# A graph layer and a mixture of 64 experts on one core: tokens laid 32 to a partition, z made by two engines, beta added to the adjacency chunk on the Pool

## The chip, the core and the metric

The kernel runs on one core of one Trainium2 chip. The metric is the device time of one execution in microseconds (us), and lower is better. A profiled execution gives a trace beside it. Engines are named PE (TensorE), DVE (VectorE), ACT (ScalarE), POOL (GpSimd) and SP (SyncE, which here only issues DMAs).

## The reference

`x` is 4096 tokens of 128 floats, `adj` is 4096 by 4096 floats.

```python
z = (x - mean(x)) / sqrt(var(x) + 1e-5)
scale = 1 / (adj.sum(1) + beta)
x = x + (scale[:, None] * (adj @ z + beta[:, None] * z)) @ kernel + bias
z1 = the same normalisation of x
logits = z1 @ Wr + br                      # 64 experts
top2, index = top_k(logits, 2)
gates = softmax(top2)
x = x + sum over the two experts e of gate[e] * (relu(z1 @ W1[e] + b1[e]) @ W2[e] + b2[e])
```

The hidden width is 256. All of it is float32; the two choices of a token decide which experts it goes to.

## The kernel before, in words

**Tiles.** 4096 tokens are 32 tiles of 128. Tile t holds tokens 128t to 128t+127, one to a partition. Four tiles are a group g (8 groups). The adjacency comes as 8 x 8 chunks of 1 MB, `adj_t[g, k]`: for the 512 target tokens of group g, the 512 source tokens of tiles 4k to 4k+3. A ring of 5 slots holds them (`load_chunk`, L324). SP waits until the chunk five before is used, and then loads the next.

**Group 0 (L847).** The layer norm of x goes first. DVE does it in steps of 4 or 8 tiles (`norm_x`, L590: statistics, a root by ACT, then one tensor_scalar a tile, L600). The last column of z is set to 1, so that the same product also sums the rows of adj. PE runs the chunks of group 0 as float32 products (`whole_chunk`, L825) as tiles of z come.

**Groups 1 to 7.** Of each group's eight chunks, seven are split. ACT rounds the chunk to `high` (`round_chunk`, L494), DVE makes the rest, `low` (`low_part`, L610, instruction L615), and PE runs three products with z_hi and z_lo (`split_chunk`, L833). There are three buffers for high and low. The eighth is a `whole_chunk`. Between the chunks of group g, PE does the rest of group g-1 by a list of places in `step`, L855: `gnn` behind tile 2, `turn_z1` at 16, `router` at 20, `ranks` at 26.

**The own product.** beta times z is added as four 128x128 products of `zi` (a copy of the group's z) with `diag` (identity times beta), behind the group's chunks (`own_product`, L819). POOL makes both (`own_rows`, L434, instructions L437 and L438), two groups ahead.

**DVE's order in group g (L674 on).** residual(g-1), low_part 3, shifts(g-1), low_part 4, 5 and 6, choose(g-1), low_part 0 of the next group, place(g-1), low_parts 1 and 2 of the next. `choose` (L640) finds the two experts and the one-hot `mask`, `place` (L658) the row numbers (`slot`, L667) from the ranks that PE has made and the counts of the tokens already seen.

**ACT's order in group g.** copy_agg(g-1), round_chunk 3, root, 4, normalise(g-1) (z1 into `payload`, L516), 5, copy_z1t, 6, then 0 to 2 of the next group.

**POOL's order.** Constants; per group the bias into x (`add_bias`, L419) and z_lo (`low_z`, L424); own_rows(0) and own_rows(1); then for each g own_rows(g+2) and dispatch(g). `dispatch` (L441) copies z1 for the second choice, waits for the pads and the slots, issues 8 indirect DMAs (L451) that scatter the tokens' rows to the experts' places in `rows`, waits until they have landed, and frees one of two payload buffers.

**Pads.** SP writes the first 128 rows of each expert's place with a row that is marked as no answer: 8 DMAs between chunk loads of groups 1 and 2 (`PADS`, L353), the last behind chunk (2, 6). No scatter starts before all have landed (`prefilled`).

**The rest.** A list of (expert, rows) tiles is made (L692 on), then 92 tiles of 128 rows go through the two expert products (L891 on), answers are scattered back to HBM and gathered in the tokens' order, scaled by the gates and written (L770, L775, L580).

```python
for g in range(GROUPS):
    if g + 2 < GROUPS:
        own_rows(g + 2)
    dispatch(g)
```

## Time and profile before

| | us |
|---|---|
| median of 3 runs | 433.78 (432.93 to 433.87) |
| the profiled execution | 433.03 |
| its span in the trace | 431.2 |
| PE busy | 359.3 |
| DVE busy | 312.4 |
| POOL busy | 250.3 |
| ACT busy | 157.8 |

Times inside the trace count from the span's start. Busy times of engines overlap, so none of them is the length of a stage; the end of a stage is set by the wait that ends last in it. "Idle before" of a row names who ended it. PEclk is the clock granted to TensorE as a part of full speed.

### The profile page before, as it was taken

Reading aid. Unit: us, or ns where it says so; the run is one execution under the profiler, and the core shown is the slowest. Engines: PE = TensorE matmul, PEld = TensorE weight load, DVE = VectorE, ACT = ScalarE, POOL = GpSimd, SP = SyncE. Lnnn points to the kernel's source line nnn. Section 1 sums busy time; section 2 is a strip of 40 time slices with the busy share of each in tenths; the row PEclk is TensorE's granted clock in tenths of the full one; section 3 lists DMA queues with packets and bytes.
Section 4 is the critical chain, followed back from the end, with each engine's and each line's share of the span. In section 5 each row is a group of like instructions: output and inputs, shape, how many; then the busy total and the mean of one; then the engine's idle time right before and its main releaser. Section 6 shows DMA issues by size and latency. Waiting matters only on the chain.

```text
span 431.2 us, 8273 instructions
## 1 busy us (share of the span) xinstructions
PE 359.3 (83%) x2029; PEld 286.2 (66%) x2029; DVE 312.4 (72%) x891; ACT 157.8 (37%) x242; POOL 250.3 (58%) x226
## 2 busy tenths in 40 slices
PE   5899699996999999999899935289999999999300
PEld 2334486784786877868678632179999999999300
DVE  2699779859789798898897628246777767677257
ACT  1115185454384654845738030001222112122054
POOL 4377600308488585884857763517777777777700
PEclk8799899996999999999999975869999999999955
DMA  8998999899696996969955110479999999997189
GB/s 267 351 423 280 338 364 357 240 361 397 249 397 218 420 366 234 401 214 403 374 218 238 44 46 19 142 205 269 307 295 311 304 285 312 295 277 235 31 288 297
DMA packets 59653, 119.32 MB, mean 277 GB/s; under 512 B 7656, under 2 KB 36604, under 8 KB 51440
## 3 DMA queue, kind: packets, MB, share of 16 engines
q1 hardware_dynamic: 41968, 95.95, 63.8%
q10 hardware_dynamic: 12672, 14.58, 11.0%
q0 software_dynamic: 4992, 8.54, 5.5%
q8 instruction: 9, 0.15, 0.1%
q14 instruction: 12, 0.10, 0.1%
HBM read 104.09 MB, written 16.78 MB: 280 GB/s over the span
## 4 chain that ended last, share of the span: by engine, by line
PE 33%; POOL 19%; DVE 17%; DMA 15%; issue 10%; ACT 3%; SPq 1%; ACTq 0%; POOLq 0%; DVEq 0%
POOL dispatched_rows L451 14%; PE bank L897 8%; DMA dispatched_rows<-payload,slot 7%; PE bank L907 4%; PE bank_pair L907 4%; DVE z_sb L600 4%; DVE adj_low L615 3%; POOL diag L438 3%; DMA x_sb<-x 3%; DMA expert_answers<-adj_ring,ans 3%; PE bank L891 2%; PE bank L843 2%; PE bank L839 2%; PE bank_pair L904 2%; PE bank L840 2%
## 5 line engine op out<-in xcount | busy, mean ns | idle before, releaser
L615 DVE TENSOR_TENSOR adj_low<-adj_ring,adj_high 128x2048 fp32r<-128x2048 f32 x49 | 114.3, 2347 | 24.5 <-ACT adj_high L501 24.2
L451 POOL DMA_INDIRECT dispatched_rows<-payload,slot x64 | 95.7, 1495 | 37.8 <-issue 31.3
L501 ACT CAST adj_high<-adj_ring 128x2048 fp32r<-128x2048 f32 x49 | 93.4, 1907 | 60.7 <-PE bank L843 47.6
L470 POOL DMA_INDIRECT expert_answers<-adj_ring,ans x92 | 90.5, 983 | 41.4 <-ACT adj_ring L551 21.8
L839 PE MATMUL bank<-adj_high,z_hi 128*128 128x512 f32 x196 | 80.7, 412 | 0.0
L840 PE MATMUL bank<-adj_high,z_lo 128*128 128x512 f32 x196 | 77.5, 396 | 0.0
L749 DVE TENSOR_SCALAR adj_ring<-bank,adj_ring 128x128 f32<-128x128 f32 x184 | 56.1, 346 | 16.4 <-PE bank L897 13.2
L829 PE MATMUL bank<-adj_ring,z_sb 128*128 128x512 f32 x120 | 58.2, 629 | 5.5 <-DVE z_sb L600 5.3
L897 PE MATMUL bank<-xt_sb,adj_ring 128*128 128x128 f32 x368 | 57.6, 280 | 0.2 <-DVE xt_sb L739 0.2
L843 PE MATMUL bank<-adj_low,z_hi 128*128 128x512 f32 x196 | 53.5, 395 | 0.0
L897 PEld LDWEIGHTS bank<-xt_sb,adj_ring 128*128 128x128 f32 x368 | 49.7, 196 | 0.5 <-DVE xt_sb L739 0.5
L829 PEld LDWEIGHTS bank<-adj_ring,z_sb 128*128 128x128 f32 x120 | 23.4, 201 | 35.5 <-issue 26.8
L437 POOL COPY zi<-z_sb 128x512 f32<-128x512 f32 x8 | 12.2, 1525 | 57.2 <-DMA dispatched_rows<-payload,slot 29.2
L843 PEld LDWEIGHTS bank<-adj_low,z_hi 128*128 128x128 f32 x196 | 37.4, 191 | 8.2
L840 PEld LDWEIGHTS bank<-adj_high,z_lo 128*128 128x128 f32 x196 | 37.5, 191 | 6.7
L839 PEld LDWEIGHTS bank<-adj_high,z_hi 128*128 128x128 f32 x196 | 37.5, 191 | 6.6
L551 ACT COPY adj_ring<-bank_pair 128x128 f32<-128x128 f32 x46 | 11.5, 266 | 76.9 <-PE bank_pair L907 47.0
L891 PE MATMUL bank<-ident,adj_ring 128*128 128x128 f32 x92 | 26.1, 286 | 9.2 <-DMA adj_ring<-dispatched_rows 8.9
L739 DVE COPY xt_sb<-bank 128x128 f32<-128x128 f32 x92 | 25.7, 280 | 10.3 <-PE bank L891 10.0
L907 PE MATMUL bank_pair<-adj_ring 128*128 128x128 f32 x184 | 28.9, 280 | 0.3 <-DVE adj_ring L749 0.3
L907 PE MATMUL bank<-adj_ring 128*128 128x128 f32 x184 | 28.4, 276 | 0.4 <-DVE adj_ring L749 0.4
L744 DVE TENSOR_TENSOR ans<-adj_ring,skip_tab 128x1 int32<-128x1 f32 x92 | 14.4, 156 | 18.0 <-DMA expert_answers<-adj_ring,ans 15.6
(125 smaller groups left out, 452.8 us busy)
## 6 DMA issues: line engine op xcount, KB each, us to landing
adj_ring<-adj_t SPq DMA_DIRECT2D x64, 1024.0 KB, 8.4
adj_ring<-w_pack SPq DMA_DIRECT2D x48, 257.5 KB
adj_ring<-w_pack ACTq DMA_DIRECT2D x44, 257.5 KB
dispatched_rows<-pad_row SPq DMA_DIRECT2D x8, 528.0 KB, 9.8
adj_ring<-expert_answers SPq DMA_DIRECT2D x8, 512.0 KB, 7.3
adj_ring<-dispatched_rows SPq DMA_DIRECT2D x48, 66.0 KB
adj_ring<-dispatched_rows ACTq DMA_DIRECT2D x44, 66.0 KB
out<-x_sb SPq DMA_DIRECT2D x8, 256.0 KB, 5.2
```

The costliest lines, as they stand in the source:

```text
L451: pool.indirect_dma_start(rows, bass.IndirectOffsetOnAxis(ap=slot[:, b, i:i + 1], axis=0), payload[:, b, t, k, :], None).then_inc(scattere ...
L470: pool.indirect_dma_start(y_tok, bass.IndirectOffsetOnAxis(ap=ans[:, s:s + 1], axis=0), y_sb[:, s, :], None, bounds_check=N * K - 1, oob_i ...
L501: nc.scalar.copy(high[:, m % PARTS], adj_sb[:, slot_of(g, k)]).then_inc(hi_ready, 1)
L615: v.tensor_tensor(low[:, m % PARTS], adj_sb[:, slot_of(g, k)], high[:, m % PARTS].bitcast(F32), ALU.subtract).then_inc(lo_ready, 1)
L749: last = v.tensor_scalar(h_sb[:, s % DEEP, c, :], up_ps[s % 2][:, c * P:(c + 1) * P], w_sb[:, s, B1_COL + c:B1_COL + c + 1], 0.0, ALU.add, ...
L829: last = mm(agg_ps[g % 2][:], z_sb[:, k * CJ + u, :], adj_sb[:, slot_of(g, k), u, :], start=(k + u == 0), stop=False)
L839: mm(agg_ps[g % 2][:], z_hi[:, j, :], high[:, m % PARTS, u, :], start=(j == 0), stop=False)
L840: mm(agg_ps[g % 2][:], z_lo[:, j, :], high[:, m % PARTS, u, :], start=False, stop=False)
L843: last = mm(agg_ps[g % 2][:], z_hi[:, k * CJ + u, :], low[:, m % PARTS, u, :], start=False, stop=False)
L891: nc.tensor.transpose(xt_ps[s % 2][:, 0:P], xin[:, s, 0:D], ident[:]).then_inc(x_turned, 1)
L897: last = mm(up_ps[s % 2][:, c * P:(c + 1) * P], w_sb[:, s, c * P:(c + 1) * P], xt_sb[:, s % 2, :], start=True, stop=True)
L907: last = mm(y, h_sb[:, s % DEEP, c, :], w_sb[:, s, H + c * D:H + (c + 1) * D], start=False, stop=(c == HC - 1))
```

## The change

Eight things change.

1. Token p*32 + t is now row p of tile t: x, the output, the answers, beta and the adjacency are laid out so. DMAs of x and out move 2 KB runs, those of the answers 4 KB. The pads are 64-partition DMAs with runs of 8 rows (4,224 B); their number, bytes and places stay.
2. z is made in six batches of x, in the order in which group 0 now takes its chunks: (1, 2, 3, 4, 5, 6, 0, 7). DVE makes half the tiles of a batch, ACT the other half. ACT loads the table of the root at the start, and DVE no longer waits for the constants.
3. The bias is no longer added to x: it is added to the weight that multiplies the sums (column 127 of z is 1 there, so a row of the weight carries it), from `gnn_b_sb`, zero but for its last row.
4. `own_rows` and `own_product` go. POOL makes `diag` and adds it to the diagonal blocks of the chunk in the ring (`add_diag`), before ACT rounds it and PE uses it. A group's own chunk comes in position 6 (position 7 in group 7).
5. `add_diag(g + 1)` stands in `dispatch(g)`, behind the payload copies.
6. The group's counts (`more`, `seen`) are summed by POOL in `dispatch`, in two steps and a third. `mask` waits on DVE for the counts of the group before, and so do the ranks on PE.
7. `chosen` goes; the one-hot and the slots read `top_i` itself. The difference of the two logits is taken once at the end.
8. `gnn(g)` on PE waits for var1 instead of the counts.

```diff
+BATCHES = ((4, 4), (8, 4), (12, 8), (20, 8), (0, 4), (28, 4))
+X_BEFORE = (1, 3, 4, 6)
+DIAG_AT = [CHUNKS - 2] * (GROUPS - 1) + [CHUNKS - 1]
+def chunk_order(g):
+    if g == GROUPS - 1:
+        return list(range(CHUNKS))
+    others = [k for k in range(CHUNKS - 1) if k != g]
+    return others + [g, CHUNKS - 1]
...
-                        sp.dma_start(first_rows[:, padded:padded + EC],
-                                     pad_row[:, None, :].to_broadcast([P, EC, ROW])).then_inc(prefilled, 16)
-                        padded += EC
+                        start = padded // PAD_BLOCKS % 2 * E
+                        sp.dma_start(blocks[:, padded:padded + PAD_BLOCKS],
+                                     pad_rows[start:start + E, None, :].to_broadcast([E, PAD_BLOCKS, PAD_RUN * ROW])).then_inc(prefilled, 16)
+                        padded += PAD_BLOCKS
...
+            def add_diag(g):
+                k = DIAG_AT[g]
+                own.after(pool.tensor_tensor(diag[:], ident[:, None, :].to_broadcast([P, GT, P]),
+                                             beta_sb[:, group(g)].to_broadcast([P, GT, P]), ALU.mult))
+                pool.wait_ge(adj_in[slot_of(g, k)], landed(g, k))
+                chunk = adj_sb[:, slot_of(g, k)].rearrange("p u n -> p (u n)")
+                most = (CJ - 1) * (GN + P)
+                blocks = chunk[:, 0:most].rearrange("p (u n) -> p u n", u=CJ - 1)[:, :, 0:P]
+                pool.tensor_tensor(blocks, blocks, diag[:, 0:CJ - 1, :], ALU.add)
+                own.after(pool.tensor_tensor(chunk[:, most:most + P], chunk[:, most:most + P], diag[:, CJ - 1, :], ALU.add))
+                pool.sem_inc(diag_added, 1)
...
+            for b in range(len(BATCHES)):
+                low_z(b)
+            add_diag(0)
...
                 pool.tensor_copy(payload[:, b, :, 1, 0:D], payload[:, b, :, 0, 0:D])
                 own.after(pool.tensor_copy(payload[:, b, :, :, ANSWER], answer_tab[:, group(g), :]))
-                pool.wait_ge(prefilled, 16 * (E // EC))
+                if g + 1 < GROUPS:
+                    add_diag(g + 1)
+                pool.wait_ge(mask_ready, g + 1)
+                own.after(pool.tensor_tensor(more[:], mask[:, 0:2, :], mask[:, 2:4, :], ALU.add))
+                own.after(pool.tensor_tensor(more[:, 0, :], more[:, 0, :], more[:, 1, :], ALU.add))
+                pool.wait_ge(rank_done, g + 1)
+                pool.tensor_tensor(seen[:], seen[:], more[:, 0, :], ALU.add).then_inc(seen_ready, 1)
+                pool.wait_ge(prefilled, 16 * PAD_DMAS)
                 pool.wait_ge(slots_ready, g + 1)
...
-            own_rows(0)
-            own_rows(1)
             for g in range(GROUPS):
-                if g + 2 < GROUPS:
-                    own_rows(g + 2)
                 dispatch(g)
...
+            def make_z(b):
+                act.wait_ge(shift0, b + 1)
+                for t in act_half(b):
+                    nc.scalar.activation(z_sb[:, t, 0:D - 1], x_sb[:, t, 0:D - 1], ACT.Identity,
+                                         bias=shift0_sb[:, t:t + 1], scale=rstd0[:, t:t + 1]).then_inc(z_by_act, 1)
...
                 act.wait_ge(adj_in[slot_of(g, k)], landed(g, k))
+                if k == DIAG_AT[g]:
+                    act.wait_ge(diag_added, g + 1)
...
-                differ = v.tensor_tensor(diff[:, group(g)], top[:, :, 1], top[:, :, 0], ALU.subtract)
-                own.after(v.tensor_copy(chosen[:], top_i[:, :, 0:K]))
+                if g > 0:
+                    dve.wait_ge(seen_ready, g)
                 v.tensor_tensor(mask[:], hot[:, :, 0, :], hot[:, :, 1, :], ALU.add).then_inc(mask_ready, 1)
...
-                own.after(v.tensor_reduce(more[:], mask[:].rearrange("p t e -> p e t"), AX_X, ALU.add))
-                v.tensor_tensor(seen[:], seen[:], more[:], ALU.add).then_inc(seen_ready, 1)
...
-            v.tensor_tensor(gnn_wd[:, 0:D], gnn_w_sb[:], wrow_ps[:, 0:D], ALU.subtract).then_inc(wd_ready, 1)
+            own.after(v.tensor_tensor(gnn_wd[:, 0:D], gnn_w_sb[:], wrow_ps[:, 0:D], ALU.subtract))
+            v.tensor_tensor(gnn_wd[:, 0:D], gnn_wd[:, 0:D], gnn_b_sb[:], ALU.add).then_inc(wd_ready, 1)
...
                 pe.wait_ge(adj_in[slot_of(g, k)], landed(g, k))
+                if k == DIAG_AT[g]:
+                    pe.wait_ge(diag_added, g + 1)
...
-            def own_product(g):
-                pe.wait_ge(own_ready, g + 1)
-                for t in range(GT):
-                    last = mm(agg_ps[g % 2][:, t * P:(t + 1) * P], zi[:, t, :], diag[:, t, :], start=False, stop=(t == GT - 1))
-                last.then_inc(agg_done, 1)
```

## Rows read from the trace of the kernel before

**Rows 1.** The page's chain of waits, shares of the span by engine.

```profile
PE 33%; POOL 19%; DVE 17%; DMA 15%; issue 10%; ACT 3%; SPq 1%; ACTq 0%; POOLq 0%; DVEq 0%
```

**Rows 2.** Windows by stage: length, then busy time and (count) of each engine, PEclk, DMA, GB/s.

```profile
0.00:49.00 49.00, 38.33 (x85) 15.15 (x86) 36.35 (x105) 12.06 (x14) 29.41 (x40) 0.93 0.92 334
...
49.30:78.00 28.70, 27.86 (x126) 21.90 (x126) 22.73 (x45) 16.09 (x14) 2.19 (x2) 0.94 1.01 332
...
78.00:111.00 33.00, 28.97 (x128) 22.24 (x127) 25.76 (x47) 16.17 (x14) 16.22 (x12) 0.90 0.92 317
...
221.00:248.80 27.80, 26.95 (x130) 20.86 (x128) 20.17 (x44) 10.47 (x11) 17.38 (x13) 1.00 0.44 173
...
248.80:282.00 33.20, 12.79 (x55) 7.12 (x55) 13.75 (x66) 4.63 (x9) 16.94 (x20) 0.73 0.23 71
```

**Rows 3.** Timeline of POOL, groups 0 to 7: start us, length us, engine, line.

```profile
96.85 2.71 POOL L451 DMA_INDIRECT dispatched_rows<-payload,slot  x1 [14.23 <-issue]
...
151.80 2.77 POOL L451 DMA_INDIRECT dispatched_rows<-payload,slot  x1 [0.28 <-POOL payload L445]
...
174.32 0.61 POOL L437 COPY zi<-z_sb 128x512 f32<-128x512 f32 x1 [5.28 <-DMA dispatched_rows<-payload,slot]
...
204.63 1.03 POOL L438 TENSOR_TENSOR diag<-ident,beta_sb 128x512 f32<-128x512 f32 x1
...
219.23 3.00 POOL L451 DMA_INDIRECT dispatched_rows<-payload,slot  x1 [0.30 <-issue]
...
250.03 0.97 POOL L451 DMA_INDIRECT dispatched_rows<-payload,slot  x1 [0.28 <-POOL payload L445]
...
261.32 0.61 POOL L444 COPY payload<-payload 128x512 f32<-128x512 f32 x1 [1.48 <-DMA dispatched_rows<-payload,slot]
```

**Rows 4.** Timeline of the start, all engines.

```profile
9.48 10.13 PE L829 MATMUL bank<-adj_ring,z_sb 128*128 128x512 f32 x16 [3.41 <-DVE z_sb L600]
...
19.24 6.08 DVE L600 TENSOR_SCALAR z_sb<-x_sb,mv,rstd 128x127 f32<-128x127 f32 x8
...
33.28 10.86 PE L829 MATMUL bank<-adj_ring,z_sb 128*128 128x512 f32 x24
...
48.35 1.31 PE L822 MATMUL bank<-diag,zi 128*128 128x128 f32 x8 [4.21 <-POOL diag L438]
```

**Rows 5.** Windows at the start of stage 1, columns as in rows 2.

```profile
48.30:52.60 4.30, 4.25 (x19) 3.86 (x20) 2.15 (x1) 0.59 (x1) 2.19 (x2) 0.61 1.12 318
...
52.60:60.00 7.40, 7.40 (x35) 6.18 (x34) 5.58 (x17) 4.53 (x5) 0.00 (x0) 1.00 1.00 399
```

**Rows 6.** Groups of instructions: busy us, mean ns, idle before.

```profile
L822 PE MATMUL bank<-diag,zi 128*128 128x128 f32 x64 | 8.7, 280 | 4.2 <-POOL diag L438 4.2
...
L422 POOL TENSOR_TENSOR x_sb<-x_sb,gnn_b_sb 128x512 f32<-128x512 f32 x8 | 10.2, 1280 | 14.6 <-DMA br_sb<-br 12.4 <-DVE z_sb L600 2.2
...
L660 DVE TENSOR_REDUCE more<-mask 128x64 f32<-128x256 bf16 x8 | 4.8, 602 | 0.1
```

**Rows 7.** ACT, DVE in stages 7 and 6, and the chain before the last scatters.

```profile
234.34 1.92 ACT L501 CAST adj_high<-adj_ring 128x2048 fp32r<-128x2048 f32 x1
...
236.29 2.29 DVE L615 TENSOR_TENSOR adj_low<-adj_ring,adj_high 128x2048 fp32r<-128x2048 f32 x1 [0.42 <-ACT adj_high L501]
...
241.51 0.43 DVE L656 TENSOR_TENSOR mask<-hot 128x256 bf16<-128x256 f32 x1
...
214.21 0.42 DVE L656 TENSOR_TENSOR mask<-hot 128x256 bf16<-128x256 f32 x1
...
219.03 0.17 DVE L667 SCALAR_TENSOR_TENSOR slot<-chosen,rank 128x8 int32<-128x8 f32 x1
...
266.20 0.73 issue
```

**Rows 8.** Timeline of stage 1: PE's first product, ACT's z1 into payload.

```profile
49.31 0.78 PE L839 MATMUL bank<-adj_high,z_hi 128*128 128x512 f32 x1
...
59.40 1.65 ACT L516 ACTIVATE payload<-x_sb,shift,rstd 128x128 f32<-128x128 f32 x4
```

More of the change, by code:

```diff
@@ L50, with batch_of, half_made, dve_half @@
 RING = 5
+BATCHES = ((4, 4), (8, 4), (12, 8), (20, 8), (0, 4), (28, 4))
+X_BEFORE = (1, 3, 4, 6)
+DIAG_AT = [CHUNKS - 2] * (GROUPS - 1) + [CHUNKS - 1]
 OUT_CH = 4
 OUT_STEPS = TILES // OUT_CH
+def batch_of(j):
+    return next(b for b, (first, count) in enumerate(BATCHES) if first <= j < first + count)
+def half_made(b):
+    return sum(count // 2 for _, count in BATCHES[:b])
+def dve_half(b):
+    first, count = BATCHES[b]
+    return range(first, first + count // 2)
+def act_half(b):
+    first, count = BATCHES[b]
+    return range(first + count // 2, first + count)
+def z_made(j):
+    b = batch_of(j)
+    if j in dve_half(b):
+        return "dve", half_made(b) + j - dve_half(b)[0] + 1
+    return "act", half_made(b) + j - act_half(b)[0] + 1
+def high_tiles(b):
+    first, count = BATCHES[b]
+    return range(first, min(first + count, SPLIT * CJ))
+def chunk_order(g):
[3 more added lines that the diff above has]
+    return others + [g, CHUNKS - 1]
 def chunk_no(g, k):
@@ L167, in program @@
         seen = sb("seen", [P, E], BF16)
-        more = sb("more", [P, E])
+        more = sb("more", [P, 2, E], BF16)
         diff = sb("diff", [P, TILES])
@@ L210, in program @@
         y_in = in_ring(TILES * K * D, "p (t k f) -> p t k f", t=TILES, k=K)
-        x_first = sem("x_first")
-        x_in = sem("x_in")
+        x_in = [sem(f"x_in{b}") for b in range(len(BATCHES))]
         params_in = sem("params_in")
@@ L399, in _ @@
             pool.memset(seen[:], 0.0)
-            pool.memset(eps_sb[:], EPS)
-            own.after(pool.memset(payload[:], 0.0))
-            pool.memset(pad_row[:, ANSWER:ANSWER + 1], float(NO_ANSWER))
+            own.after(pool.memset(payload[:, :, :, :, ANSWER + 1:ROW], 0.0))
             pool.affine_select(out=ident[:], in_=ident[:], compare_op=ALU.not_equal, fill=1.0, base=0,
@@ L429, in _, with low_z @@
-            for g in range(GROUPS):
-                add_bias(g)
-                if g < SPLIT:
-                    low_z(g)
-            def own_rows(g):
-                if g > 0:
-                    pool.wait_ge(agg_done, g)
-                pool.tensor_copy(zi[:], z_sb[:, group(g), :])
-                pool.tensor_tensor(diag[:], ident[:, None, :].to_broadcast([P, GT, P]),
-                                   beta_sb[:, group(g)].to_broadcast([P, GT, P]), ALU.mult).then_inc(own_ready, 1)
+            def low_z(b):
+                tiles = high_tiles(b)
+                if not tiles:
+                    return
+                pool.wait_ge(z_hi_ready, b + 1)
+                for first in range(tiles[0], tiles[-1] + 1, GT):
+                    quad = slice(first, first + GT)
+                    pool.tensor_tensor(z_lo[:, quad, :], z_sb[:, quad, :], z_hi[:, quad, :].bitcast(F32),
+                                       ALU.subtract).then_inc(z_lo_ready, 1)
@@ L475, in _, with root_z, high_z @@
         def _(act):
[L476 to L492 removed]
+            act.wait_ge(eps_ready, 1)
+            nc.scalar.activation(std[:, 0:1], eps_sb[:], ACT.Sqrt)
+            act.wait_ge(z_ones, 1)
+            def root_z(b):
+                first, count = BATCHES[b]
+                act.wait_ge(var0, b + 1)
+                nc.scalar.activation(root0[:, first:first + count], mv0[:, first:first + count, 1], ACT.Sqrt,
+                                     bias=eps_sb[:]).then_inc(std0, 1)
+            def make_z(b):
[3 more added lines that the diff above has]
+                                         bias=shift0_sb[:, t:t + 1], scale=rstd0[:, t:t + 1]).then_inc(z_by_act, 1)
+            def high_z(b):
+                tiles = high_tiles(b)
+                if not tiles:
+                    return
+                act.wait_ge(z_by_act, half_made(b + 1))
+                act.wait_ge(z_by_dve, half_made(b + 1))
+                nc.scalar.copy(z_hi[:, tiles[0]:tiles[-1] + 1, :], z_sb[:, tiles[0]:tiles[-1] + 1, :]).then_inc(z_hi_ready, 1)
+            root_z(0)
+            for b in range(len(BATCHES)):
+                make_z(b)
+                if b + 1 < len(BATCHES):
+                    root_z(b + 1)
+                high_z(b)
             def round_chunk(g, k):
@@ L689, in _ @@
             place(GROUPS - 1)
+            v.tensor_tensor(diff[:], top[:, :, 1], top[:, :, 0], ALU.subtract).then_inc(diff_ready, 1)
             dve.wait_ge(total_done, 1)
```

182 lines of the change are left out of this document (90 added, 92 removed).

## Prediction

> **What bounds the kernel now.** I read the chain of waits first, then the stages by window, then each engine's timeline. The chain gives PE a third of the span, POOL a fifth and DVE a sixth [rows 1]; no one engine owns the end. The stages say where. I call stage g the stretch in which PE runs the eight chunks of group g. Stage 0 and the wait behind it last to 49 us; the steady stages last 27 to 28 us with PE busy for all but about one of them [rows 2], so PE sets the pace there, at full clock. Stage 2 takes 33 us because DMA is full: its share is 0.92 to 1.01 in the first three stages.
>
> POOL stands close behind PE. One turn of its scatters, from the first DMA_INDIRECT to the moment when POOL is free again, lasts 151.80 to 174.32, 22.5 us (16 to 17 us of issues, 5.28 us for the landing) [rows 3]. It runs late: the first turn waits for the pads until 96.85 [rows 3], long after its slots were there, and the turns behind it follow back to back. This costs little now, for nobody needs POOL soon: `own_rows(g + 2)` stands ahead of `dispatch(g)`, two groups before its product, and payload has two buffers. The lateness is covered by that distance. After PE's last chunk, 33.2 us pass before the experts start; what follows is PE's and DVE's, and the change leaves it as it is but for the length of runs in the output's transfers [rows 2].
>
> **The start.** DVE makes all of z. Eight z tiles took 6.08 us [rows 4] while POOL added the bias beside them; PE waited, then waited 4.21 us more for `diag` (48.35). The change halves DVE's share of z, takes the bias off POOL, loads the square-root table early and drops the own product. Three chunks in a row cost PE 10.86 us [rows 4], so 3.6 us each and 29 us for eight. They start near 6 us, when the warm-up products are done, instead of at 9.48 [rows 4]; the last chunks land at about 2.6 us a megabyte (399 GB/s [rows 5]), near 30 us. With beta's additions (below) I put the start of stage 1 at 36 us instead of 49.31: **13 us earlier**. It is no gain at the end unless the next two points let it through.
>
> **The own product and small steps.** Removed: the eight products of each group on PE (64 of 280 ns, pipelined, about 1 us a group [rows 6]), POOL's copy of zi, the DVE reduction of `mask` (0.60 us, L660 [rows 6]), its sum and two small operations of about 0.17 us. If PE stayed the bound, 7 x 1.0 = 7 us would go. Added on POOL: three small sums, and beta's additions: L422 adds 128x512 in 1.28 us [rows 6], so 384 and 128 columns are 0.96 + 0.35 us. They wait until z is finished in stage 0, and cost about 1 us there.
>
> **Where the additions stand.** This is the large term. `add_diag(g + 1)` stands inside `dispatch(g)`, so behind all scatters of `dispatch(g - 1)` and their landing. It changes a chunk that lies in position 6 of the group now on PE, and ACT's rounding of that chunk waits for it. DVE's queue has `low_part(g, 6)` in front of `choose` and `place`, so the slots, which POOL needs for its next scatters, wait for it too. This closes a loop with nothing two groups ahead in it. One turn, piece by piece:
> - addition done to slots. ACT's rounding at 234.34, DVE's low at 236.29, then the choice to the end of the mask at 241.94 [rows 7]: 7.6 us; the two small steps leave 7.3. Mask to slots in stage 6, with a low_part between: 214.63 to 219.20, 4.57 us [rows 7]; less 0.60 and 0.22 it is 3.8. Together 11.1 us.
> - slots to first scatter: 0.75 us (266.20 to 266.93 [rows 7]).
> - the turn of scatters: 22.5 us as now. Alone, without large DVE operations, eight issues take 9.8 us (250.03 to 259.85) and the landing 1.5 us, 11.3 us in all [rows 3]. The new turn starts as DVE enters five or six low_parts, and an issue beside them took 3.00 us instead of 0.96 [rows 3], so I take the 17 us of issues; DMA is less loaded by then (8.4 MB in a longer stage), so 3 us for the landing: 20 us.
> - payload copies 0.6 + 0.2, `diag` 1.03 [rows 3], additions 1.3, waits 0.3: 3.5 us, DVE being idle.
>
> The sum is 11.1 + 0.75 + 20 + 3.5 = **35.4 us** a stage instead of 27.3 to 28. A second loop bounds it below: from an addition PE needs about 13.2 us to the next stage (234.34 to the end of stage 7 at 248.8 is 14.4 us; the own product and the small steps leave 13.2) and z1 is there 11.7 us after a stage's start (49.31 to 61.05 [rows 8]); with 3.5 us that is 28.4. The turn as long as now gives 37.9. So 28.4 to 37.9, and 35.4 is nearest to turns beside low_parts.
>
> On the landing of pads: 64-partition runs of 4,224 B replace 528 B rows, whose price I can only bound. About 30 MB must have landed before the last pad; at 399 GB/s that is 77 us plus the start, at the 332 GB/s of stage 1 it is 92. I take 80, for the pads were the slow share. The last pad's load must also wait for stage 1. `dispatch(0)` scatters from 80: 10 to 12 us of issues, as DVE is blocked meanwhile by the missing addition, and 3 to land; then 3.5 us. The addition of group 2 is done at about 97 us; stage 2 (from 36 + 28 = 64 us; ACT rounds position 6 about 13 us into a stage, 221 to 234.34 [rows 2, 7]) would have wanted it near 77. **The 13 us of the start are lost here**: the pads set it.
>
> Then additions 3 to 6 follow at 35.4 us each: 97 + 141.6 = 238.6. Group 7 has its diagonal in position 7, whole, and does not hold up choose. PE has 14 us to its stage's start and 27 us of work to its end, or 41 us, longer than POOL's. So its last chunk ends at 280 us, against 247.9 now: +32. The way from there to the experts is 33.2 us [rows 2] less 1 us of DVE; the output's loads and stores have longer runs, which I put at -1.5 us, between none and -3, since the work of DVE and ACT between them stays. Net **+29.5 us**. The profiled execution took 433.03 us, 1.8 us around a span of 431.2 and 0.75 us under the median of the runs, 433.78. So 433.0 + 29.5 = 462.5; I say 462.
>
> **A rule against a row.** Scatter issues stretch beside DVE's L615, from 0.96 to 3.00 us [rows 3]. The Trainium skill, SBUF — State Buffer, section "Who interferes with whom", says that `tensor_tensor` has no two-port mode and infers that it does not hold up descriptor generation; by that rule the turn would be 11.3 us anywhere. This trace disagrees.
>
> **Rivals.**
> - *Short turns.* If the issues keep 0.96 us each while DVE is held back, the turn is 11.3 us, the loop 26.7 and z1's bound of 28.4 decides: 97 + 4 x 28.4 + 41 = 251.6, that is 433.0 + 3.7 - 2.5 = 434. With the pads at 72 instead of 80, it is 426, and from that pad time on this rival ends faster. For: the issues at 250. Against: every turn with low_parts beside it [rows 3]. Chance 0.09: 0.06 faster (the pads come a little early as well), 0.02 the same, 0.01 slower. The page's rule above would give this one.
> - *No loop at all*, if POOL's waits fit into PE's stages: 36 + 7 x 26.3 = 220, 28 us less than now, and about 403 us. It decides if a turn is below 10 us. Chance 0.02.
> - *Long turns and a slow clock.* The turn stays at 22.5, and PE, which then idles 9 us in each stage (35.4 less 26.3), comes back at half its clock: after the 4.21 us wait the granted clock was 0.61 over 4.3 us [rows 5], that is 1.2 GHz for most of it. 10 us more for four turns and 3 for the clock: 475. Chance 0.2.
> - *The pads as late as now* (97 instead of 80): 17 us more, 479, but for the turns' shorter landing; a pad at 70 gives 452. These two are edges of the forecast.
>
> **How the numbers follow.** The loop with 31 to 37.9 us a turn has 0.69 and the long turns 0.2: 445 to 475, and 3 us more at both ends for the pads. Below the range lie the two short cases. A measurement of this kernel tells 0.2% (about 0.9 us) from no change. Faster is 0.06 of the short turns and 0.02 of no loop, together 0.08; same 0.02; slower the other 0.9.
>
> **What would show it.** Right: ACT's rounding in position 6 waits 8 us or more for POOL in stages 2 to 6; PE idles there as long; the distance between two stages' ends is 33 to 38 us; the first scatters at about 80; stage 1 starts near 36 us; L451 issues average above 1.3 us. Wrong: steady stages of 26 to 28 us, POOL waiting for z1 ahead of its additions, or the first scatter before 70 us.

## The result, and the profile after the change

The changed kernel takes 479.54 us (median of 4 runs, 472.74 to 480.61) against 433.39 us: a ratio of 1.098, 95% interval 1.086 to 1.110, so 46 us slower. Forecast were 462 us and a range of 442 to 478: the direction held, the size was 17.5 us short and the median lies 1.5 us above the range. The profiled execution took 478.73 us with a span of 476.9 us.

The page's chain of waits by engine answers to [rows 1], and two of its groups of instructions (busy us, mean ns, idle before and what ended it) stand behind it:

```profile
PE 33%; DMA 18%; DVE 15%; POOL 15%; issue 10%; ACT 5%; SPq 2%; POOLq 1%; ACTq 0%; DVEq 0%
...
L521 POOL DMA_INDIRECT dispatched_rows<-payload,slot x64 | 92.4, 1444 | 48.7 <-DMA dispatched_rows<-pad_rows 21.2
...
L700 DVE TENSOR_TENSOR adj_low<-adj_ring,adj_high 128x2048 fp32r<-128x2048 f32 x49 | 112.8, 2302 | 87.6 <-ACT adj_high L582 87.3
```

The scatter issues themselves are no longer than before (1444 ns against 1495). New is DVE's 87.6 us of waiting for ACT's rounded chunks, 24.5 us before. DVE's busy time fell from 312.4 to 295.6 us: the work was taken off, and the engine stands idle instead.

The windows by stage, columns as in [rows 2]:

```profile
39.00:75.00 36.00, 29.64 (x121) 22.38 (x120) 26.86 (x43) 17.82 (x16) 8.73 (x8) 0.91 0.86 329
...
75.00:122.70 47.70, 28.81 (x118) 21.62 (x117) 23.44 (x42) 15.91 (x15) 17.30 (x18) 0.79 0.58 223
...
122.70:157.50 34.80, 27.31 (x118) 20.62 (x117) 22.99 (x42) 16.05 (x14) 18.55 (x17) 0.90 0.64 255
...
268.70:295.00 26.30, 25.57 (x117) 19.28 (x115) 16.66 (x38) 10.37 (x11) 18.95 (x18) 1.00 0.47 182
...
295.00:329.00 34.00, 13.76 (x57) 7.73 (x58) 12.99 (x64) 4.63 (x9) 15.07 (x19) 0.73 0.27 83
```

Stages 3 to 6 last 34.8, 39.5, 35.4 and 36.3 us where they were 27 to 28. Stage 7, whose addition holds up the last chunk only, lasts 26.3 us with PE busy for 25.6 of it, which is what PE needs without the own product. Stage 2 lasts 47.7 us. The last product of group 7 ends at 295.0 us instead of 247.9; the way to the experts (34.0 against 33.2) and the experts themselves are unchanged, so all of the loss stands in stages 1 to 6.

What PE waits for, from the table of who waited for whom (total, times, longest):

```profile
ACT adj_high L582 <- POOLq L498: 35.2, 5, 10.4
...
PE bank L919 <- ACT adj_high L582: 32.3, 5, 15.6
```

ACT waited 35.2 us in five times for POOL's additions (3.1 us in stage 1, then 7.1, 10.4, 7.3 and 7.2 in stages 3 to 6). A sixth wait of ACT, in stage 2, stands in its timeline as 18.49 us of "issue", with POOL's 103.81 to 107.16 in front of its end. PE waited 32.3 us in five times for ACT, 15.6 us in stage 2 and 3.3 to 6.5 us in each of stages 3 to 6; there it waited 3.3 to 4.2 us more for the mask, which comes behind the addition. One turn of the loop, from the timelines of POOL, ACT and DVE, addition of group 2 to addition of group 3:

```profile
106.71 0.45 POOL L497 TENSOR_TENSOR adj_ring<-adj_ring,diag 128x128 f32<-128x128 f32 x1
...
107.28 5.50 ACT L582 CAST adj_high<-adj_ring 128x2048 fp32r<-128x2048 f32 x3 [18.49 <-issue]
...
109.22 2.29 DVE L700 TENSOR_TENSOR adj_low<-adj_ring,adj_high 128x2048 fp32r<-128x2048 f32 x1 [18.58 <-ACT adj_high L582]
...
114.15 0.42 DVE L737 TENSOR_TENSOR mask<-hot 128x256 bf16<-128x256 f32 x1
...
118.20 0.17 DVE L745 SCALAR_TENSOR_TENSOR slot<-top_i,rank 128x8 int32<-128x8 uint32 x1
...
119.15 2.32 POOL L521 DMA_INDIRECT dispatched_rows<-payload,slot  x1 [1.31 <-DVE slot L745]
...
131.88 2.43 POOL L521 DMA_INDIRECT dispatched_rows<-payload,slot  x1 [0.31 <-issue]
...
139.31 0.61 POOL L508 COPY payload<-payload 128x512 f32<-128x512 f32 x1 [4.99 <-DMA dispatched_rows<-payload,slot]
...
142.20 0.45 POOL L497 TENSOR_TENSOR adj_ring<-adj_ring,diag 128x128 f32<-128x128 f32 x1
```

The addition is done at 107.16. ACT rounds the chunk (107.28), DVE makes its low part (109.22), the mask is done at 114.57, the slots at 118.37. The first scatter starts at 119.15, the last issue ends at 134.31, the landing takes 4.99 us more, POOL is free at 139.31 and has added again at 142.65. In the pieces of the prediction, from addition done to slots 11.2 us (11.1 forecast), to the first scatter 0.78 (0.75), the turn of scatters 20.2 (20), to the next addition done 3.3 (3.5), together 35.5. The next three loops are 38.1, 36.5 and 35.2 us; their turns of scatters took 22.8, 21.1 and 19.9 us. The mean of the four is 36.3.

### The profile page after: what moved, and what is told of

Same layout as the page of the kernel before. It is cut to its first block, busy times and chain, and to the rows that moved or that the text cites. A ratio compares the mean times of both kernels' runs of the same rounds, so it can differ in the third digit from the quotient of the medians.

```text
span 476.9 us, 8177 instructions
## 1 busy us (share of the span) xinstructions
PE 365.7 (77%) x1965; PEld 287.2 (60%) x1965; DVE 295.6 (62%) x852; ACT 163.3 (34%) x261; POOL 246.5 (52%) x251
## 4 chain that ended last, share of the span: by engine, by line
PE 33%; DMA 18%; DVE 15%; POOL 15%; issue 10%; ACT 5%; SPq 2%; POOLq 1%; ACTq 0%; DVEq 0%
POOL dispatched_rows L521 11%; PE bank L980 8%; DMA adj_ring<-adj_t 7%; DMA dispatched_rows<-payload,slot 7%; DVE adj_low L700 6%; ACT adj_high L582 4%; PE bank L990 4%; PE bank_pair L990 4%; PE bank L909 4%; PE bank L923 2%; DMA expert_answers<-adj_ring,ans 2%; PE bank L974 2%; PE bank_pair L987 2%; PE bank L987 2%; PE bank L919 2%
## 5 line engine op out<-in xcount | busy, mean ns | idle before, releaser
L700 DVE TENSOR_TENSOR adj_low<-adj_ring,adj_high 128x2048 fp32r<-128x2048 f32 x49 | 112.8, 2302 | 87.6 <-ACT adj_high L582 87.3
L521 POOL DMA_INDIRECT dispatched_rows<-payload,slot x64 | 92.4, 1444 | 48.7 <-DMA dispatched_rows<-pad_rows 21.2
L919 PE MATMUL bank<-adj_high,z_hi 128*128 128x512 f32 x196 | 87.6, 447 | 32.3 <-ACT adj_high L582 32.3
L920 PE MATMUL bank<-adj_high,z_lo 128*128 128x512 f32 x196 | 81.4, 415 | 0.0
L919 PEld LDWEIGHTS bank<-adj_high,z_hi 128*128 128x128 f32 x196 | 39.5, 202 | 43.1 <-ACT adj_high L582 34.4
L923 PE MATMUL bank<-adj_low,z_hi 128*128 128x512 f32 x196 | 57.6, 419 | 0.0
L923 PEld LDWEIGHTS bank<-adj_low,z_hi 128*128 128x128 f32 x196 | 40.6, 207 | 9.5
L920 PEld LDWEIGHTS bank<-adj_high,z_lo 128*128 128x128 f32 x196 | 39.7, 202 | 8.7 <-issue 1.7
L909 PEld LDWEIGHTS bank<-adj_ring,z_sb 128*128 128x128 f32 x120 | 24.5, 206 | 31.5 <-issue 27.3
L513 POOL TENSOR_TENSOR more<-mask 128x128 bf16<-128x128 bf16 x8 | 15.3, 1912 | 50.3 <-DVE mask L737 50.3
L974 PE MATMUL bank<-ident,adj_ring 128*128 128x128 f32 x92 | 26.3, 286 | 9.1 <-DMA adj_ring<-dispatched_rows 8.8
L508 POOL COPY payload<-payload 128x512 f32<-128x512 f32 x8 | 5.5, 683 | 48.9 <-DMA dispatched_rows<-payload,slot 26.1
```

What stands on the lines that cost most here:

```text
L521: pool.indirect_dma_start(rows, bass.IndirectOffsetOnAxis(ap=slot[:, b, t, k:k + 1], axis=0), payload[:, b, t, k, :], None).then_inc(scatt ...
L700: v.tensor_tensor(low[:, m % PARTS], adj_sb[:, slot_of(g, k)], high[:, m % PARTS].bitcast(F32), ALU.subtract).then_inc(lo_ready, 1)
L909: last = mm(agg_ps[g % 2][:], z_sb[:, j, :], adj_sb[:, slot_of(g, k), u, :], start=(k + u == 0), stop=(k + 1 == CHUNKS and u + 1 == CJ))
L919: mm(agg_ps[g % 2][:], z_hi[:, first + u, :], high[:, m % PARTS, u, :], start=(k + u == 0), stop=False)
L920: mm(agg_ps[g % 2][:], z_lo[:, first + u, :], high[:, m % PARTS, u, :], start=False, stop=False)
L923: last = mm(agg_ps[g % 2][:], z_hi[:, first + u, :], low[:, m % PARTS, u, :], start=False, stop=False)
```

## Experiments

The theory: the additions stand in POOL's queue behind the scatters of the group before, the slots of the next scatters wait for the addition, and this loop sets the length of a stage. The rivals: the rest of the change costs something (counts on POOL, adding into the chunk at all), or late pads, clock or DMA make the stages long and POOL's wait is where it shows.

### One part undone: the own product back

`add_diag` and its waits go out of the changed kernel; zi, diag, `own_rows(g + 2)` ahead of `dispatch(g)` and the four products on PE come back.

```diff
-                if g + 1 < GROUPS:
-                    add_diag(g + 1)
...
+            own_rows(0)
+            own_rows(1)
             for g in range(GROUPS):
+                if g + 2 < GROUPS:
+                    own_rows(g + 2)
                 dispatch(g)
...
                     (split_chunk if is_split(g, k) else whole_chunk)(g, k, step)
+                own_product(g)
```

> The changed kernel with beta's part alone undone: zi, diag, the own product on PE and own_rows two groups ahead as before; layout, z by two engines, bias in the weight and the counts on POOL stay. Loop theory: no wait of ACT on POOL is left, steady stages of 27 to 28 us, the scatters lag again behind PE without cost, and the earlier start shows: 415 to 425 us. Rival (the other parts of the change cost something themselves, above all the counts on POOL that mask and ranks wait for): 433 or more.

Measured: 421.47 us, ratio to the kernel before 0.972 (0.964 to 0.980). Run again with five rounds, it took 421.17 us, 0.972 (0.967 to 0.976). Its windows by stage:

```profile
41.30:68.50 27.20, 26.41 (x126) 20.33 (x125) 23.13 (x41) 16.70 (x15) 3.69 (x2) 1.00 1.00 408
...
68.50:98.50 30.00, 28.11 (x128) 21.80 (x127) 24.26 (x42) 16.39 (x15) 16.45 (x15) 0.94 0.89 352
...
98.50:125.50 27.00, 26.44 (x127) 20.52 (x127) 22.41 (x42) 16.10 (x14) 19.85 (x15) 1.00 0.85 334
...
207.00:234.00 27.00, 26.43 (x126) 20.44 (x124) 17.93 (x39) 10.38 (x11) 21.76 (x21) 1.00 0.44 176
```

Steady stages are 27.0 us with PE busy for 26.4 of them. The one part is worth 58 us: the change without it is faster than the kernel before, and the rival that the other parts make the loss falls (a small loss by the counts alone is looked at below). POOL's scatters are late in this kernel too (the first at 84.79; 96.85 in the kernel before), and neither ACT nor PE waits for them.

### The same part done alone, in the kernel before

```diff
+DIAG_AT = [CHUNKS - 2] * (GROUPS - 1) + [CHUNKS - 1]
...
-            own_rows(0)
-            own_rows(1)
+            own_rows(0)
             for g in range(GROUPS):
-                if g + 2 < GROUPS:
-                    own_rows(g + 2)
                 dispatch(g)
...
+                if g + 1 < GROUPS:
+                    add_diag(g + 1)
                 pool.wait_ge(prefilled, 16 * (E // EC))
```

> The kernel before with beta's part alone done for groups 1 to 7: the group's own chunk in position 6 (7 in the last), add_diag(g + 1) inside dispatch(g), no own product there. Nothing else of the change. Loop theory: 35 to 37 us between two additions and, since stage 1 starts 10 us later than in the changed kernel, 475 to 490 us. Rival (the loss comes from the sum of small steps in the change): under 445.

Measured: 497.17 us, 1.145 (1.135 to 1.155), beyond the expected band on the theory's side. The additions of groups 2 and 3 end with

```profile
117.94 0.45 POOL L461 TENSOR_TENSOR adj_ring<-adj_ring,diag 128x128 f32<-128x128 f32 x1
...
154.54 0.45 POOL L461 TENSOR_TENSOR adj_ring<-adj_ring,diag 128x128 f32<-128x128 f32 x1
```

and those of groups 2 to 6 are done at 118.4, 155.0, 193.8, 230.3 and 268.6 us, 37.6 us apart in the mean. The loop alone makes the loss and more. The 17.6 us to the changed kernel are the later addition of group 2 (118.4 against 107.2, 11.2 us), four loops that are 1.3 us longer (5.0 us), and 1.3 us in the last group.

### The landing taken out of the loop

```diff
                     add_diag(g + 1)
+                if g > 0:
+                    pool.wait_ge(scattered, g * (GT * K * 16))
+                    pool.sem_inc(payload_free, 1)
                 pool.wait_ge(mask_ready, g + 1)
...
-                pool.wait_ge(scattered, (g + 1) * (GT * K * 16))
-                pool.sem_inc(payload_free, 1)
```

> The changed kernel, with POOL's wait for the landing of group g-1's scatters moved from the end of dispatch(g-1) to behind add_diag(g) inside the next dispatch. Loop theory (the additions stand behind the scatters, and that loop sets the length of stages 2 to 6): the landing, 4.9 to 5.2 us a turn in the changed kernel's trace, leaves four loops and 2 us of it the first turn, so about 22 us less: 457 us, and 31 us between two additions instead of 36.3. Rival (the stages are long because PE runs at half its clock or because chunks arrive late, and POOL's wait is only where it shows): within 3 us of the changed kernel's 478.7.

Measured: 463.54 us, 1.066 (1.058 to 1.075): 16 us less than the changed kernel, not 22. POOL's timeline, the addition of group 2, the first and last scatter behind it, the next payload copy and the next addition:

```profile
106.51 0.45 POOL L497 TENSOR_TENSOR adj_ring<-adj_ring,diag 128x128 f32<-128x128 f32 x1
...
118.96 2.31 POOL L524 DMA_INDIRECT dispatched_rows<-payload,slot  x1 [1.32 <-DVE slot L746]
...
134.01 3.07 POOL L524 DMA_INDIRECT dispatched_rows<-payload,slot  x1 [0.30 <-issue]
...
137.08 0.62 POOL L508 COPY payload<-payload 128x512 f32<-128x512 f32 x1
...
140.01 0.46 POOL L497 TENSOR_TENSOR adj_ring<-adj_ring,diag 128x128 f32<-128x128 f32 x1
```

The landing is gone from between the last issue and the payload copy, but this loop is 33.5 us, not 31: its issues take 18.1 us (118.96 to 137.08) where they took 15.2. Four loops average 33.3, 3.0 us less than in the changed kernel. The theory stands in kind, since nothing but POOL's waiting was moved and the loop followed. Of the 5.0 us of landing, 2.1 came back. One half is in the issues: a turn has 16.9 us of them in the mean of four, 15.9 in the changed kernel. The other half is in the copies: in the third and fourth turn the copy of `answer_tab` (L509) takes 2.27 us where it took 0.19, for it now falls beside a low_part of DVE (202.02 beside 201.69).

### The slots taken out of the loop

Each group's own chunk goes to position 7, the whole one, for all groups from 1 on. `add_diag` stays behind the scatters, but `low_part(g, 6)`, choose and place no longer wait for it.

```diff
-DIAG_AT = [CHUNKS - 2] * (GROUPS - 1) + [CHUNKS - 1]
+DIAG_AT = [CHUNKS - 2] + [CHUNKS - 1] * (GROUPS - 1)
...
-    others = [k for k in range(CHUNKS - 1) if k != g]
-    return others + [g, CHUNKS - 1]
+    if g == 0:
+        return list(range(1, CHUNKS - 1)) + [0, CHUNKS - 1]
+    return [k for k in range(CHUNKS) if k != g] + [g]
...
-        z_hi = sb("z_hi", [P, SPLIT * CJ, D], F32R)
-        z_lo = sb("z_lo", [P, SPLIT * CJ, D], F32R)
+        z_hi = sb("z_hi", [P, TILES, D], F32R)
+        z_lo = sb("z_lo", [P, TILES, D], F32R)
```

> The changed kernel with each group's own chunk in position 7, the whole one, in all groups from 1 on (z_hi and z_lo for all 32 tiles). add_diag stays where it is in POOL's queue, behind the scatters. The slots no longer wait for the addition: low_part(g, 6), choose and place run without it. Loop theory: of the 36.3 us the 11 us from addition to slots leave the loop and POOL's own work stays (20.2 us of scatters and landing, 3 of sums, 3.5 to 5 of additions), so 26 to 29 us a stage and 432 to 445 us in all. Rival (any wait of PE or ACT for an addition behind scatters costs the same): within 10 us of 479.

Measured: 447.73 us, 1.029 (1.021 to 1.037). That is 32 us less than the changed kernel, which excludes the rival, and 3 us above the band. POOL's timeline says why the band was missed:

```profile
106.15 0.45 POOL L498 TENSOR_TENSOR adj_ring<-adj_ring,diag 128x128 f32<-128x128 f32 x1
...
108.38 1.02 POOL L522 DMA_INDIRECT dispatched_rows<-payload,slot  x1 [0.41 <-issue]
...
123.18 0.92 POOL L509 COPY payload<-payload 128x512 f32<-128x512 f32 x1 [4.84 <-DMA dispatched_rows<-payload,slot]
...
128.47 2.51 POOL L498 TENSOR_TENSOR adj_ring<-adj_ring,diag 128x128 f32<-128x128 f32 x1
...
133.82 2.41 POOL L514 TENSOR_TENSOR more<-mask 128x128 bf16<-128x128 bf16 x1 [2.83 <-DVE mask L738]
...
138.31 2.32 POOL L522 DMA_INDIRECT dispatched_rows<-payload,slot  x1 [1.31 <-DVE slot L746]
...
162.95 0.61 POOL L509 COPY payload<-payload 128x512 f32<-128x512 f32 x1 [5.29 <-DMA dispatched_rows<-payload,slot]
...
169.77 0.45 POOL L498 TENSOR_TENSOR adj_ring<-adj_ring,diag 128x128 f32<-128x128 f32 x1
```

The additions are 24.1 to 24.9 and 39.1 to 39.2 us apart by turns. The one done at 131.0 comes before the mask, so POOL waits 2.83 us for the mask, starts its scatters at 138.31, and is free at 162.95. The ones done at 106.6 and 170.2 come after the mask, and the scatters start at once. The larger part of the difference is what the turns run beside: the eight issues from 138.31 take 19.4 us beside DVE's low_parts, those from 108.38 take 9.95 us. The mean over five intervals is 30.3 us, against 26 to 29 expected. The way from addition to slots was the part of the loop that the place in the chunk's order decided, and POOL's own queue the rest.

### The pads

The last pad of the changed kernel stands behind load (2, 6) in SP's queue. From the timelines of SP and POOL:

```profile
74.94 0.34 SPq L389 DMA_DIRECT2D adj_ring<-adj_t  x1
...
79.55 0.82 SPq L412 DMA_DIRECT2D dispatched_rows<-pad_rows  x1
...
91.78 1.15 POOL L521 DMA_INDIRECT dispatched_rows<-payload,slot  x1 [21.17 <-DMA dispatched_rows<-pad_rows]
...
103.81 0.61 POOL L508 COPY payload<-payload 128x512 f32<-128x512 f32 x1 [2.05 <-DMA dispatched_rows<-payload,slot]
```

The load at 74.94 is (2, 4). It takes the slot of chunk (1, 7), the whole chunk, so it waited for the end of stage 1 (the expectation for the moved pads names (2, 6) for this, which only stands behind it in the queue). A pad, and two more loads with a pad each, stand behind it, and the last pad, issued at 79.55, ends POOL's wait at 91.78. Between the end of stage 1 (ACT's agg_sb copy) and the first scatter lie 16.8 us here (74.94 to 91.78), 15.8 with the own product back (69.01 to 84.79), 16.8 with the additions on DVE (70.59 to 87.38), and with the pads in 528 B rows 18.5 in the kernel before (78.38 to 96.85) and 19.6 with the addition alone (84.03 to 103.58). The first scatter follows the end of stage 1.

```diff
-PADS = ((0, 0, 1, 0, 1, 0, 0, 1), (0, 1, 0, 1, 1, 1, 1, 0))
+PADS = ((1, 1, 1, 1, 1, 1, 1, 1), (0, 0, 0, 0, 0, 0, 0, 0))
```

> The changed kernel with all eight pad DMAs behind the eight chunk loads of group 1, so none in group 2. In the changed kernel the last pad was issued at about 80 and landed at 91.5; its place is behind load (2, 6), which waits for chunk (1, 7) to be used, the end of stage 1. Theory (the first turn of scatters waits for that place, not for the bytes): the pads land before the slots are there (71 to 76), the addition of group 2 comes at 95 to 99 instead of 107, and the loops behind it keep their 36 us: 466 to 472 us. Rival (the bytes decide, so the pads land near 90 in either place, or the eight loads starve stage 1 by as much): 476 or more.

Measured: 471.27 us, 1.085 (1.077 to 1.093), inside the theory's band for the time; the addition of group 2 comes 0.8 us behind its band of 95 to 99. The first scatter and the end of the addition of group 2:

```profile
73.60 2.30 POOL L521 DMA_INDIRECT dispatched_rows<-payload,slot  x1 [1.46 <-DVE slot L745]
...
99.38 0.45 POOL L497 TENSOR_TENSOR adj_ring<-adj_ring,diag 128x128 f32<-128x128 f32 x1
```

The first scatter starts 18 us earlier, as soon as the slots are there. The addition comes only 7.3 us earlier (99.83 against 107.16), since this turn now runs beside DVE's low_parts and the chunk loads: 17.8 us of issues instead of 10, and a landing of 5.03 us at a DMA share of 1.01 instead of 2.05 us at 0.11. The time follows the addition.

```diff
-    return range(first, first + count // 2)
+    return range(first, first + count)
...
-                act.wait_ge(z_by_act, half_made(b + 1))
```

> The changed kernel with all of z made by DVE, so that stage 1 starts later by as much as in e7_own_z_dve. The prediction had the start's gain lost because the pads' bytes set the first scatters. If so, the additions of groups 2 to 7 stay within 1 us of the changed kernel's 107, 142, 180, 217, 252 and the time near 479. Rival (the last pad is issued behind the end of stage 1, so a later start moves everything): the first scatter and all additions move with the start, one to one.

Measured: 481.70 us, 1.109 (1.103 to 1.114). This one could not tell much: with all of z on DVE the end of stage 1 moved by 0.6 us (75.54) and the first scatter by 0.6 (92.35). Both followed together, but the step is too small to decide; the row of five kernels above and the moved pads do.

### The other parts

z by two engines, undone in the kernel with the own product (edit as above):

> e2_own_product with all of z made by DVE again, in the six batches; ACT keeps roots and rounding. Nothing else. If z by two engines is what shortens the start: stage 1 starts 3 to 6 us later than the 39 us there and the whole is 3 to 6 us longer than 417 to 421. Rival (the chunks' arrival sets stage 0, z is hidden): within 1.5 us.

Measured: 422.15 us, 0.972 (0.968 to 0.975), against 421.5 and 421.2: the rival holds. PE's products of group 0 begin at 9.5 us and the own product at 40.2, with two engines at 9.8 and 40.5.

The bias, undone in the same kernel:

```diff
+            for b in range(len(BATCHES)):
+                add_bias(b)
                 low_z(b)
...
-            v.tensor_tensor(gnn_wd[:, 0:D], gnn_wd[:, 0:D], gnn_b_sb[:], ALU.add).then_inc(wd_ready, 1)
```

> e2_own_product with the bias added to x on POOL again, one 128x512 sum for every four tiles beside DVE's z, and taken out of the weight. Theory (the earlier start of stage 1, 39 to 41 us against 49.3, comes from POOL's freed queue: no sums beside DVE's z tiles, so zi and diag are there when PE wants them): PE's last product of group 0 ends 3 to 7 us later and the whole is 3 to 7 us over e2_own_product's 417 to 422. Rival (the batches and the order of loads make the start): within 1.5 us of it.

Measured: 423.72 us, 0.978 (0.972 to 0.983), some 2.4 us over its base with intervals that meet: unclear. POOL had diag ready at 37.5 us, ahead of PE's 40.83, so the start did not move by the 3 to 7 us expected. Neither of the two alone makes the earlier start; the two together were not undone. What is left of it, the batches with the statistics of the next one ahead, the order of the loads and DVE's start without the constants, was not undone either. So which part starts stage 1 some 8 to 10 us earlier stays open.

The counts, back on DVE:

```diff
-                own.after(pool.tensor_tensor(more[:], mask[:, 0:2, :], mask[:, 2:4, :], ALU.add))
-                own.after(pool.tensor_tensor(more[:, 0, :], more[:, 0, :], more[:, 1, :], ALU.add))
...
+                own.after(v.tensor_reduce(more[:, 0, :], mask[:].rearrange("p t e -> p e t"), AX_X, ALU.add))
```

> The changed kernel with the counts (more, seen) back on DVE as before; the additions stay on POOL inside dispatch. Loop theory: the three sums on POOL end in the trace before the slots are there, so they take nothing from the loop, while DVE gets back 0.60 + 0.22 us between mask and slots: four loops longer by 0.5 to 0.9 us, 479 to 484 us. Rival (the counts on POOL hold the scatters back, 2.4 us for the first sum): 470 or less.

In the changed kernel: 481.46 us, 1.109 (1.103 to 1.115), its loops 36.2, 38.2, 37.8 and 37.0 us (the mean, 37.3, is 1.0 above 36.3). The 2.41 us of POOL's first sum hold nothing up: with the counts on DVE the first scatter starts 12.8 us behind the addition of group 2 (106.46 to 119.22), with them on POOL 12.0 (107.16 to 119.15).

> e2_own_product with the counts on DVE again, so that of the change only the layout, the batches, z by two engines and the bias in the weight are left. In its trace PE waits for the mask 8.5 us in all and POOL's turns are back to back only until group 5. If the counts on POOL gain by their 0.8 us a group between mask and slots, which PE's ranks do not wait for: no change within 2 us of e12_own_product_again, run on the same chip. Rival (DVE is near enough to the bound that 6.6 us more on it show): 3 to 7 us more.

In the kernel with the own product: 418.30 us, 0.964 (0.960 to 0.967), against 0.972 (0.967 to 0.976) for its base on the same chip. By the medians the counts are better on DVE, by 3 us, which neither side of the expectation had, and the intervals just miss each other (0.9670 and 0.9673); the profiled executions say the opposite (spans of 418.8 and 416.2). No gain from the counts on POOL is shown, and a small loss is not excluded.

> e2_own_product once more, on the same chip as e11_own_counts_dve, with five rounds: 417 to 423 us and a narrower interval, to set it beside e5_dve_adds (0.962 of the kernel before, 0.9595 to 0.965). If adding on DVE is no better than the own product, the two intervals overlap.

Measured: 421.17 us, inside the band, with the interval given above (0.967 to 0.976).

### A version that beats both

beta's addition on DVE, between low_part 4 and 5, one operation a block:

```diff
+            def add_diag(g):
+                k = DIAG_AT[g]
+                dve.wait_ge(adj_in[slot_of(g, k)], landed(g, k))
+                for t in range(GT):
+                    block = adj_sb[:, slot_of(g, k), t, t * P:(t + 1) * P]
+                    last = v.scalar_tensor_tensor(out=block, in0=ident[:], scalar=beta_sb[:, g * GT + t:g * GT + t + 1],
+                                                  in1=block, op0=ALU.mult, op1=ALU.add)
+                own.after(last)
+                dve.sem_inc(diag_added, 1)
...
                 low_part(g, 4)
+                if g < GROUPS - 1:
+                    add_diag(g)
```

> The changed kernel with beta's addition moved from POOL to DVE: four scalar_tensor_tensor operations (identity times beta plus block) between low_part(g, 4) and low_part(g, 5), behind low_part 6 in the last group. No own product on PE, nothing of POOL's queue in front of ACT. Loop theory: stages of 26 to 27 us (27.0 in e2_own_product less 1.0 of own product, if the 1.2 us that DVE gets fit beside PE), and 405 to 415 us, under e2_own_product. Rival (adding into the chunk itself costs more than the own product, wherever it is done, since ACT and PE wait for it): 420 or more.

Measured: 418.33 us, 0.962 (0.960 to 0.965), just above the expected band and 3.8% under the kernel before. Two steady stages, and the new operation in the groups of instructions:

```profile
102.30:128.80 26.50, 25.54 (x118) 19.65 (x117) 22.74 (x46) 16.26 (x14) 17.49 (x14) 1.00 0.86 338
...
181.50:207.60 26.10, 25.54 (x118) 19.64 (x117) 24.55 (x46) 16.14 (x15) 17.62 (x14) 1.00 0.87 343
```

```profile
L684 DVE SCALAR_TENSOR_TENSOR adj_ring<-ident,beta_sb,adj_ring 128x128 f32<-128x128 f32 x32 | 10.2, 378 | 7.9 <-DMA adj_ring<-adj_t 7.9
```

Stages of 26.1 to 26.5 us: the own product's 1 us is gone from PE, and DVE's 32 x 378 ns fit beside it. Adding into the chunk costs nothing that these stages show; adding there from a queue with scatters in it did. The whole gains less than 8 x 1 us over the own product, for stage 2 got longer (31.7 against 30.0 us) and stage 7 lasts 27.4; against the repeated run, on another chip, the intervals are apart (0.960 to 0.965, 0.967 to 0.976). But this version has the counts on POOL, and the own product with the counts on DVE is as good (418.30 us, 0.964, interval 0.960 to 0.967). So it is shown to beat the kernel before and the changed one, and not to be the best of those tried.

## Why the prediction was right, and where it was short

- **The loop: right.** Place, members and price: 36.3 us measured, 35.4 forecast. The term that was short is the turn of scatters, 21.0 us in the mean of four instead of 20, and inside it two errors met. The landing did not shrink to 3 us but stayed at 4.9 to 5.2, and the issues took 15.9 us instead of 17. The step "DMA is less loaded by then" spoke of the stage's mean, which did fall to 0.6; in the stretch of the landing itself the share was 1.02 (rows in the last section). That the two nearly cancel is luck. The whole was worth 3.6 us.
- **The first scatter: wrong, the largest term.** "On the landing of pads" put it at 80, by bytes through DMA; it came at 91.8. The step said that the last pad's load "must also wait for stage 1" and priced nothing for it. In SP's queue three pads stand behind load (2, 4), which takes the slot of the whole chunk (1, 7), so they cannot be issued before the end of stage 1, and POOL's wait for them ended 12.2 us behind the last issue. Stage 1 ended at 74.9 instead of 64: it began at 39.0 instead of 36, and it lasted 36 us instead of 28. PE waits 2.59 us in it for the copy of agg_sb (to 43.12) and 3.77 us for the mask, which stands behind stage 1's own addition (59.9 us), and is busy for the other 29.6 us, at a granted clock of 0.91. From the first scatter to the addition of group 2 it was 15.4 us, not 17, so that addition was 10.2 us late (107.2 against 97).
- **"The 13 us of the start are lost here": not so.** The pads follow the end of stage 1, and that follows the start. The kernel with the addition alone shows it: stage 1 ends 9.1 us later than in the changed one, the first scatter 11.8 us, the addition of group 2 11.2 us.
- **The start: 39.0 instead of 36.** PE's first product came at 9.43 us, not 6. Its tiles of z belong to the first batch, whose root ACT had ready at 5.76 us, but on DVE they stand behind the statistics of the second batch, which wait for its x:

```profile
7.47 0.88 DVE L672 BATCH_NORM_STATS2 stats<-x_sb 128x6 f32<-128x128 f32 x4 [2.11 <-DMA x_sb<-x]
...
8.94 0.60 DVE L686 TENSOR_SCALAR z_sb<-x_sb,mv,rstd 128x127 f32<-128x127 f32 x2
```

  The causes named (half of z on ACT, no bias on POOL) moved nothing each by itself.
- **The last group.** 42.6 us from the last loop's addition to PE's end instead of 41: 1.6 us. From there to the end 2.5 us less were forecast and 1.4 came (181.9 us behind 295.0, 183.3 behind 247.9 before): 1.1 us. The forecast took the end of PE's last chunk at 247.9 and the way from there at 248.8; between them lies the own product of group 7.
- **The sum.** Of the profiled execution these are 10.2 + 3.6 + 1.6 + 1.1 = 16.5 us, less 0.3 of rounding (279.6 was taken as 32 us behind 247.9): the 16.2 us between 478.73 and the 462.5 worked out. The forecast said 462 and the median is 479.54, which makes the 17.5 us.
- **The signs.** Stages of 33 to 38 us came in three of five (34.8, 35.4, 36.3; 39.5 and 47.7 did not), and the issues averaged 1.44 us. The wait of ACT, "8 us or more", came in stages 2 and 4 alone; in the others it was 7.1 to 7.3 us. PE did not idle as long as ACT: 3.3 to 6.5 us for ACT in stages 3 to 6, and 3.3 to 4.2 us for the mask.
- **Rivals.** Short turns did not come. The turn of 21.0 us lies between the 20 of the forecast and the 22.5 of the long turns. The clock rival was right that PE comes back slowly (granted clock 0.79 in stage 2, 0.83 to 0.90 in stages 3 to 6). In the loop read above this cost little: the way from addition to slots, in which PE has its part, took 11.2 us against 11.1. The number it gave, 475, was close for another reason.

**The rule and the row.** The forecast set a rule against a row, and the row held. Issues of the changed kernel alone, then beside DVE, then POOL's first sum beside a low_part and in the last group without one:

```profile
198.21 0.97 POOL L521 DMA_INDIRECT dispatched_rows<-payload,slot  x1 [0.30 <-issue]
...
203.31 2.62 POOL L521 DMA_INDIRECT dispatched_rows<-payload,slot  x1 [0.30 <-issue]
...
188.27 2.41 POOL L513 TENSOR_TENSOR more<-mask 128x128 bf16<-128x128 bf16 x1 [7.50 <-DVE mask L737]
...
309.15 0.42 POOL L513 TENSOR_TENSOR more<-mask 128x128 bf16<-128x128 bf16 x1 [4.89 <-DVE mask L737]
```

A DVE low_part and a scatter issue, from the timeline of all engines:

```profile
194.77 2.29 DVE L700 TENSOR_TENSOR adj_low<-adj_ring,adj_high 128x2048 fp32r<-128x2048 f32 x1 [0.59 <-ACT adj_high L582]
...
195.38 2.52 POOL L521 DMA_INDIRECT dispatched_rows<-payload,slot  x1 [0.30 <-issue]
```

The issue at 195.38 ends 0.84 us after the low_part that began at 194.77 (it ends at 197.06). The Trainium skill, SBUF — State Buffer, section "Who interferes with whom", infers that `tensor_tensor` does not hold up the descriptors of POOL's DMAs. Issues of 0.97 us alone and mostly 1.8 to 3.1 us beside it, in every trace read here, say that something in the issue is held up. Whether it is the descriptors or the reading of the row numbers from `slot`, no run here tells. The same section says that a DVE operation with two SBUF inputs contends with a POOL operation that reads SBUF; that agrees with the sum: the 128x128 sum takes 2.41 us beside L700 and 0.42 without.

## What to carry to other kernels

When a small operation moves into another engine's queue, write down what stands in front of it there, to the last wait, and what that wait needs in its turn: here 1.4 us of additions closed a loop of 36 us. A queue may run late for free only as long as nothing near is asked of it; `own_rows(g + 2)` ahead of `dispatch(g)` was that licence, and the change gave it up. And ask what a transfer's place in its queue waits for before counting bytes: with the pads in another place, and not a byte less, the first scatter came 18 us earlier.

## What was not expected of the hardware

The landing of eight scatters kept its 4.9 to 5.2 us although the DMA share of a stage fell from 0.85 to 0.6. Windows laid over the landings alone, columns as in [rows 2], show a different share there. At 134.31 and at 101.76:

```profile
134.31:139.31 5.00, 5.00 (x30) 4.27 (x29) 2.29 (x1) 0.88 (x2) 0.01 (x2) 1.00 1.02 428
...
101.76:103.81 2.05, 0.00 (x0) 0.00 (x0) 0.00 (x0) 0.00 (x0) 0.00 (x1) 0.50 0.11 37
```

In all four landings of the changed kernel's loops the share is 1.02, as in the landing at 169.04 of the kernel before (5.28 us). Where it is 0.11 to 0.14, a landing takes 1.5 to 2.05 us, and 2.4 us at 0.52. No run moved the loads alone, so this is a row of readings and not a test; but a stage's mean share says little about one transfer in it.

And moving the landing out of the loop lengthened one turn's issues from 15.2 to 18.1 us in the same place, 15.9 to 16.9 in the mean of four: a scatter issue has no price of its own, it has one by what DVE does meanwhile.
